# Turning the normalised rows on the DMA queues and VectorE instead of on TensorE

## The reference

```python
h = jnp.maximum(_layernorm(x, axis=-1), 0.0)
x = x + _L0_gnn_ref(h, adj, ...)
h = jnp.maximum(_layernorm(x, axis=-1), 0.0)
x = x + _L1_gnn_ref(h, adj, ...)
# _L0_gnn_ref
Xw = X @ Wv + bv
sj = Xw @ aw[:d, 0]
si = Xw @ aw[d:, 0]
e = jax.nn.leaky_relu(sj[:, None, :] + si[:, :, None] + ab[0], negative_slope=0.2)
alpha_matrix = A * jnp.exp(e)
transition = alpha_matrix / (jnp.sum(alpha_matrix, axis=-1, keepdims=True) + 1e-12)
for k in range(Wk.shape[0]):          # K = 3
    H = H + Xk @ Wk[k] + bk[k]
    Xk = jnp.einsum('bij,bjd->bid', transition, Xk)
return jax.nn.relu(H)
# _L1_gnn_ref: three times  x <- adj @ (x @ W) + b, with relu behind the first two
```

## Time and profile before

| what | value |
|---|---|
| median of 3 runs | 881.63 us (881.37 to 883.54) |
| the profiled execution | 881.72 us, its span 879.9 us |
| PE / PEld busy | 864.7 us (98%) / 817.7 us (93%) |
| DVE busy | 760.2 us (86%) |
| ACT busy | 628.2 us (71%) |
| POOL busy | 435.8 us (50%) |
| DMA queue of SP | 43.81 MB, 20.0% of 16 engines |

### The profile page before, as it was taken

One profiled execution on the slowest core, in us unless ns is written; L12 is line 12 of the kernel. 1 busy time (PEld: TensorE's weight loads), 2 busy tenths in 40 slices (PEclk: granted clock), 3 DMA queues, 4 the chain that ended last, 5 costly groups with the idle time before them and its releaser, 6 DMA issues.

```text
span 879.9 us, 20848 instructions
## 1 busy us (share of the span) xinstructions
PE 864.7 (98%) x6480; PEld 817.7 (93%) x6480; DVE 760.2 (86%) x2001; ACT 628.2 (71%) x1543; POOL 435.8 (50%) x532
## 2 busy tenths in 40 slices
PE   8899999999999999999999999999999999999996
PEld 7799999999999999999999999999999999999996
DVE  5789889889889889889889889899889889889872
ACT  4477777777777777777777777777777777777773
POOL 4454454454454454454454454454454454454452
PEclk9899999999999999999999999999999999999999
DMA  8112122122122122122122122122122122122001
GB/s 202 36 34 57 36 61 56 36 61 56 37 61 57 35 61 56 36 61 57 36 61 58 35 61 57 35 62 56 35 61 57 35 62 57 35 61 58 18 25 37
DMA packets 107869, 46.18 MB, mean 52 GB/s; under 512 B 72560, under 2 KB 107504, under 8 KB 107760
## 3 DMA queue, kind: packets, MB, share of 16 engines
q1 hardware_dynamic: 106672, 43.81, 20.0%
q10 hardware_dynamic: 1088, 1.05, 0.4%
HBM read 28.05 MB, written 16.78 MB: 51 GB/s over the span
## 4 chain that ended last, share of the span: by engine, by line
PE 95%; SPq 1%; POOL 1%; ACT 1%; issue 1%; DMA 1%; DVE 0%; DVEq 0%; ACTq 0%; POOLq 0%
PE bank L856 43%; PE bank_p L856 35%; PE bank_turned L856 7%; PE bank_T L856 5%; PE bank_turned L867 3%; PE bank_T L877 2%; SPq L261 1%; DMA bias_col<-in_L_gnn_b 1%; POOL w_gcn_lo L361 0%; PE bank_p L1012 0%; POOL bias_h L377 0%; ACT h L487 0%; ACT y_full L524 0%; DVE aT_lo L573 0%; SPq L252 0%
## 5 line engine op out<-in xcount | busy, mean ns | idle before, releaser
L334 POOL TENSOR_TENSOR y__lo<-y_full,y__hi 128x256 fp32r<-128x256 f32 x256 | 190.1, 764 | 112.3 <-ACT y_full L524 112.3
L325 POOL TENSOR_TENSOR rstd<-veps,minus_half 128x2 f32<-128x2 f32 x128 | 88.9, 695 | 236.4 <-DVE veps L596 236.4
L856 PE MATMUL bank_p<-w_p_hi,h0T_hi 128*128 128x258 f32 (+1 forms) x512 | 176.3, 360 | 0.1
L856 PE MATMUL bank_p<-w_p_lo,h0T_hi 128*128 128x258 f32 (+1 forms) x512 | 165.3, 339 | 0.0
L856 PE MATMUL bank_p<-w_p_hi,h0T_lo 128*128 128x258 f32 (+1 forms) x512 | 142.1, 339 | 0.7 <-DVE h0T_lo L629 0.7
L856 PE MATMUL bank<-w_gcn_hi,y__hi 128*128 128x256 f32 x512 | 132.8, 292 | 1.5 <-ACT y__hi L524 1.3
L856 PE MATMUL bank<-w_gcn_lo,y__hi 128*128 128x256 f32 x512 | 127.8, 282 | 0.0
L524 ACT ACTIVATE y__hi<-bank,bias_col 128x256 fp32r<-128x256 f32 x256 | 119.7, 467 | 3.0 <-PE bank L856 3.0
L524 ACT ACTIVATE y_full<-bank,bias_col 128x256 f32<-128x256 f32 x256 | 121.6, 475 | 0.0
L350 POOL TENSOR_TENSOR adjT_lo<-adjT_full,adjT_hi 128x256 fp32r<-128x256 f32 x64 | 64.9, 1015 | 82.8 <-ACT adjT_hi L429 82.8
L856 PEld LDWEIGHTS bank_p<-w_p_hi,h0T_hi 128*128 128x128 f32 x512 | 97.3, 190 | 6.2 <-POOL w_p_lo L356 0.3
(11 more groups left out here) (92 smaller groups left out, 2346.2 us busy)
## 6 DMA issues: line engine op xcount, KB each, us to landing
x_in<-in_x SPq DMA_DIRECT2D x64, 256.0 KB, 3.0
x_new<-x_out SPq DMA_DIRECT2D x64, 256.0 KB, 2.2
adj_blocks<-in_adj SPq DMA_DIRECT2D x256, 32.0 KB, 2.3
w_raw<-in_L_gnn_Wk ACTq DMA_DIRECT2D x3, 256.0 KB, 6.9
w_raw<-in_L_gnn_W SPq DMA_DIRECT2D x3, 256.0 KB, 5.5
bk_bc<-in_L_gnn_bk SPq DMA_DIRECT2D x1, 384.0 KB, 6.1
wv_raw<-in_L_gnn_Wv ACTq DMA_DIRECT2D x1, 256.0 KB, 3.8
aw_bc<-in_L_gnn_aw SPq DMA_DIRECT2D x1, 256.0 KB, 5.6
```

The costliest lines, as they stand in the source:

```text
L325: pool.tensor_tensor(rstd[n][k % 2][:], veps[n][k % 2][:], minus_half[:], ALU.pow)\
L334: pool.tensor_tensor(y[n][1][:, c], y_full[n][:, c], plain(y[n][0][:, c]), ALU.subtract)\
L856: return pe.matmul(dst, stationary, moving, start=start, stop=stop, skip_group_check=True)
```

## The change

- `turn_h` and its pair of reads from PSUM stay for the pairs 0 to 2 (`ON_TENSOR = 3`). From pair 3 on, the rows go out to DRAM with one DMA (`write_rows`) and come back in four (`read_rows`) as 32x32 squares in transposed order, pieces of 128 bytes; VectorE turns the insides with one 128x512 transpose (`turn_rows`); ScalarE makes the high part and GpSimd the low part, both in the round before the one that uses them.
- The normalised rows are made by ScalarE (`first_norm`, relu included) two rounds ahead, for which VectorE makes a small `shift(0, ...)`. VectorE's `x_norm` goes. VectorE's 128x512 `hT_low` stays for three pairs only. The moments of x are taken three pairs ahead.
- `attention` moves ahead of `shift(1, b)` on VectorE, `aT_high` ahead of `norm` on ScalarE.
- On TensorE `p2_product` is split: its 8 products with the high part come first in the round, ahead of z3 and ay; the 4 with the low part stay behind ay.
- `x_in` has five slots in place of four, and x is loaded three rounds ahead.

The diff, cut to its core (the waits of unchanged functions and renamed views of PSUM are left out; `low(...)` is a subtraction, dst = src - hi):

```diff
 ROUND = 4
+X_SLOTS = 5
 LAG_B, LAG_C, LAG_D = 1, 2, 3
+ON_TENSOR = 3
...
         rstd = [slots(2, f"rstd{n}_", [P, G]) for n in range(2)]
-        nshift = slots(2, "nshift", [P, G])
-        n0 = slots(2, "n0_", [P, G, D])
+        nshift = [slots(2, f"nshift{n}_", [P, G]) for n in range(2)]
+        h0 = slots(2, "h0_", [P, G, D])
+        h0_rows = [nc.dram_tensor(f"h0_rows{k}", (P, G, D), F32, kind="Internal").ap() for k in range(2)]
+        h0_blocks = slots(2, "h0_blocks", [P, G, C, P])
+        h0T_full = slots(2, "h0T_full", [P, G, C, P])
         h1 = slots(2, "h1_", [P, G, D])
-        h0T = slots_hilo(2, "h0T", [P, C, G, P])
+        h0T = slots_hilo(2, "h0T", [P, G, C, P])
...
+        def early_norm(i):
+            n = i + 1 if i <= 1 else i + 2
+            return n if i >= 1 and n < N_PAIRS else None
+        def late_moments(i):
+            n = 2 if i == 0 else i + 3
+            return n if n < N_PAIRS else None
+        LATE_NORMS = {0: 1, 1: 3}
...
+            def write_rows(i, k):
+                sp.wait_ge(norm_made[0], i + 1)
+                if i >= ON_TENSOR + 2:
+                    sp.wait_ge(rows_landed[k % 2], rows_seen(i - 2))
+                sp.dma_start(h0_rows[k % 2], h0[k % 2][:]).then_inc(rows_out[k % 2], 16)
+            def read_rows(i, k):
+                sp.wait_ge(rows_out[k % 2], 16 * ((i - ON_TENSOR) // 2 + 1))
+                if i >= ON_TENSOR + 2:
+                    sp.wait_ge(rows_turned, i - 2 - ON_TENSOR + 1)
+                pair = h0_rows[k % 2].rearrange("(j r) g (c i s) -> i r (g c) j s", r=SQUARE, c=C, s=SQUARE)
+                for b in range(P // SQUARE):
+                    rows = slice(b * SQUARE, (b + 1) * SQUARE)
+                    sp.dma_start(h0_blocks[k % 2][rows].rearrange("r g c (j s) -> r (g c) j s", s=SQUARE),
+                                 pair[b]).then_inc(rows_landed[k % 2], 16)
...
             def one(i, k):
+                if first(i):
+                    load_x(2)
+                if (n := here(i, -3)) is not None:
+                    load_x(n)
+                turned = here(i, -2) if i >= ON_TENSOR - 2 else None
+                if turned is not None:
+                    write_rows(turned, turned % ROUND)
                 if (n := here(i, -2)) is not None:
-                    load_x(n, (k + 2) % ROUND)
-                    load_adj_blocks(n, (k + 2) % ROUND)
+                    load_adj_blocks(n, n % ROUND)
+                if turned is not None:
+                    read_rows(turned, turned % ROUND)
...
                 pool.tensor_tensor(x1b[k][:], x1[k % 2][:], bias_out[:], ALU.add).then_inc(x1b_made, 1)
+            def hT_low(i, k):
+                pool.wait_ge(hT_hi, i + 1)
+                if after(i, 2):
+                    pool.wait_ge(p01_done, G * (i - 1))
+                hi, lo = h0T[k % 2]
+                pool.tensor_tensor(lo[:], h0T_full[k % 2][:], plain(hi[:]), ALU.subtract).then_inc(hT_lo, 1)
...
                     power(1, b, k - LAG_B)
-                if (n := here(i, -1)) is not None:
-                    power(0, n, k + 1)
+                if (n := LATE_NORMS.get(i)) is not None:
+                    power(0, n, n)
                 if first(i):
                     sum_biases()
                 if c is not None:
                     y_low(1, c, k - LAG_C)
+                if (n := here(i, -1)) is not None and n >= ON_TENSOR:
+                    hT_low(n, n % ROUND)
                 if b is not None:
                     out_bias(b, (k - LAG_B) % ROUND)
+                if (n := late_moments(i)) is not None:
+                    power(0, n, n)
...
+            def first_norm(i, k):
+                act.wait_ge(shift_made[0], i + 1)
+                if i >= ON_TENSOR + 2:
+                    act.wait_ge(rows_out[k % 2], 16 * ((i - 2 - ON_TENSOR) // 2 + 1))
+                elif i >= 2:
+                    act.wait_ge(hT_done, i - 1)
+                for g in range(G):
+                    last = act.activation(h0[k % 2][:, g, :], x_in[i % X_SLOTS][:, g, :], ACT.Relu,
+                                          bias=nshift[0][k % 2][:, g:g + 1], scale=rstd[0][k % 2][:, g:g + 1])
+                last.then_inc(norm_made[0], 1)
+            first_norm(0, 0)
...
-                act.wait_ge(hT_done, i + 1)
+                if i < ON_TENSOR:
+                    act.wait_ge(hT_done, i + 1)
+                else:
+                    act.wait_ge(rows_turned, i - ON_TENSOR + 1)
                 if after(i, 2):
                     act.wait_ge(p01_done, G * (i - 1))
-                act.activation(h0T[k % 2][0][:], turned_ps, ACT.Relu).then_inc(hT_hi, 1)
+                act.activation(h0T[k % 2][0][:], turned_ps if i < ON_TENSOR else h0T_full[k % 2][:], ACT.Copy)\
+                   .then_inc(hT_hi, 1)
...
                     layer_result(0, c)
+                if (n := early_norm(i)) is not None:
+                    first_norm(n, n % ROUND)
...
                     p1_copy(a, k, 0)
+                if a is not None:
+                    aT_high(a, k)
                 if b is not None:
                     norm(b, kb)
-                if a is not None:
-                    aT_high(a, k)
                 if c is not None:
                     layer_result(1, c)
                 if a is not None:
                     p1_copy(a, k, 1)
+                if (n := here(i, -1)) is not None and n >= ON_TENSOR:
+                    hT_high(n, n % ROUND)
...
                     adjT_high(a, k)
+                if (n := LATE_NORMS.get(i)) is not None:
+                    first_norm(n, n % ROUND)
...
                     dve.wait_ge(p01_done, G * (i - 1))
-                dve.scalar_tensor_tensor(lo[:], turned_ps, 0.0, plain(hi[:]), ALU.max, ALU.subtract)\
-                   .then_inc(hT_lo, 1)
+                low(lo[:], turned_ps, hi[:], hT_first_lo)
+            def turn_rows(i, k):
+                dve.wait_ge(rows_landed[k % 2], rows_seen(i))
+                if i >= ON_TENSOR + 2:
+                    dve.wait_ge(hT_hi, i - 1)
+                    dve.wait_ge(hT_lo, i - 1 - ON_TENSOR)
+                dve.transpose(h0T_full[k % 2][:].rearrange("p g c n -> p (g c n)"),
+                              h0_blocks[k % 2][:].rearrange("p g c n -> p (g c n)")).then_inc(rows_turned, 1)
...
                     s3_low(d)
-                if a is not None:
+                if a is not None and a < ON_TENSOR:
                     hT_low(a, k)
+                if (n := early_norm(i)) is not None:
+                    shift(0, n, n % ROUND)
...
                     turn_adj(a, k)
+                if a is not None:
+                    attention(a, k)
                 if b is not None:
-                    shift(b, kb)
-                if nxt is not None:
-                    moments(0, nxt, kn, lambda: attention(a, k))
-                    guard_variance(0, nxt, kn)
-                elif a is not None:
-                    attention(a, k)
+                    shift(1, b, kb)
+                if i == 1:
+                    x_statistics(3, 3)
+                    moments(0, 3, 3, lambda: None)
+                    guard_variance(0, 3, 3)
+                if nxt is not None and nxt >= ON_TENSOR:
+                    turn_rows(nxt, kn)
                 if d is not None:
                     finish(d, kd)
                 if a is not None:
                     aT_low(a, k)
-                if nxt is not None:
-                    x_norm(nxt, kn)
+                if i == 1:
+                    shift(0, 3, 3)
                 if a is not None:
                     guard_sum(a, k)
                     invert_sum(a, k)
-                if (n := here(i, -2)) is not None:
-                    x_statistics(n, (k + 2) % ROUND)
+                if (n := here(i, -3)) is not None:
+                    x_statistics(n, n % ROUND)
                 if a is not None:
                     y1_sum(a, k)
                 if b is not None:
                     m_low(b)
+                if (n := late_moments(i)) is not None:
+                    moments(0, n, n % ROUND, lambda: None)
+                    guard_variance(0, n, n % ROUND)
...
-            def p2_product(i, k):
+            def p2_product(i, k, low):
+                dst = [bank_p2[:, g, 0:D + 2] for g in range(G)]
+                if low:
+                    h_low_ready(i)
+                    times_weights(h0T[k % 2], graph_first, w_p2, dst, range(G), (True,)).then_inc(p2_done, 1)
+                    return
                 pe.wait_ge(hT_hi, i + 1)
                 if first(i):
                     pe.wait_ge(p2_weights_cut, 2)
                 if after(i, 1):
                     pe.wait_ge(y1_made, i)
-                times_weights(h0T[k % 2], w_p2, [bank_p2[:, g, 0:D + 2] for g in range(G)], range(G),
-                              lambda: pe.wait_ge(hT_lo, i + 1)).then_inc(p2_done, 1)
+                times_weights(h0T[k % 2], graph_first, w_p2, dst, range(G), (False,))
...
```

(33 more changed lines are left out.)

96 lines of the change are left out of this document (47 added, 49 removed).

## The result

The changed kernel takes 877.11 us (median of 8 runs, 876.72 to 880.26), the kernel before 882.05 us beside it: ratio 0.995 (95% interval 0.9939 to 0.9961). It is faster by 4.9 us, where 11.4 was forecast. The profiled execution took 879.86 us, a slow one among these 8, against 881.72 before. So the two traces show 1.9 us of the 4.9.

A forecast was written before the change was run, and what follows sets the result against it. Two bounds at once: TensorE's order (13.20 us a round) and a VectorE-TensorE ring (13.11). 881.7 + 3 for the start - 61 x 0.236 (14.4) = 870.3, said as 870.5 us; range 857 to 893 us.

The forecast's parts named there:

- The next pair's `mv` and `veps` leave this stretch: On VectorE, from hb to aT_lo: these two instructions go away from there, in a stretch summed to 6.24 us.
- the ring: Work passing from VectorE (hb to aT_lo) to TensorE (ap to ay) and back each round: 13.11 us before, 12.94 forecast.
- My own walk: GpSimd's instructions timed from hb to see whether x is held: x1b to 10.7 us, fit within 0.1 us.
- the rule on two engines excluding each other: A VectorE instruction with two SBUF inputs and a GpSimd one reading SBUF exclude each other; the second issued is blocked.
- Its VectorE part: VectorE from the start of hb to the end of aT_lo: 6.94 us before, 6.24 forecast.
- The TensorE part: TensorE from the last two ap products to the end of ay: 6.04 - 0.44 + 0.97 = 6.57 us.
- my sign for the whole: TensorE idle about 0.2 us a round before the last ap products; without a wait for aT_lo the prediction fails.
- The forecast round of 12.96: Steady round: the summed 12.94 us, taken as 12.96 for small waits left out, against 13.196 before.
- TensorE's floor: TensorE's own work in a round without the transposes: 13.20 - 0.44 = 12.76 us.
- The rival at 858 us: Chance 0.15: the VectorE-TensorE ring doesn't bind, TensorE's own 12.76 us a round does: 881.7 + 3 - 26.8.
- `x` is not held: VectorE's x free of GpSimd, 0.72 to stats; rival (chance 0.20, including other losses): x stays held, 13.37 a round, 895 us.
- The start: First rounds: GpSimd's late weights 2.0 us, p2's high products waiting for ScalarE's copy 0.9; together 3, between 0 and 6.

The follow-up runs named there:

- Experiment 1: Changed kernel with VectorE's moments of pair i+3 (mv, veps) behind s_lo instead of ahead of it: 868.13 us, ratio 0.9837.
- experiment 4: Changed kernel with VectorE's transpose of the rows behind aT_lo instead of ahead of finish and aT_lo: 876.74 us, ratio 0.9949.
- experiment 9: Changed kernel with ScalarE making pair 1's normalised rows right behind aT_high(0), not at the end of its round 0: 876.88 us, ratio 0.994.
- Experiments 1 and 5: 5, from the changed kernel: moments behind s_lo and rows' transpose behind aT_lo, 867.66 us; moments and p2's high products behind ay, 875.90; all three, 875.34.
- turn twice: Changed kernel with VectorE's 128x512 transpose of the rows done twice, the second into a spare tile: 892.87 us, ratio 1.0114.
- the two kernels with the old order: The kernel before, 882.05 us, and the same with its four transposes left out for pairs 3 to 63, 865.29 us, ratio 0.9809.

## Why the prediction was wrong

The direction and the range were right (chance of faster 0.63), the size was not: 11.4 forecast, 4.9 measured.

**The step that failed** is "The next pair's `mv` and `veps` leave this stretch." I took them off the ring at no cost and did not ask where they went. They went between `m_lo` and `s_lo`, one stretch on, and there GpSimd's `x1b` runs. My own walk had it there, from 9.4 to 10.7 us behind `hb`, where it was measured (9.39 to 10.70). I used the rule on two engines excluding each other for `x`, `y_lo` and `alpha`, and not for an instruction of two elements. It cost 1.1 us a round on VectorE, of which 0.35 reached TensorE. Experiment 1 shows it: 9 us back with that place alone. In the Trainium skill, "SBUF — State Buffer", section "Who interferes with whom", `tensor_scalar` is among the operations that can take the port pair shared with GpSimd, and "issue order, not op shape, decides who blocks". This trace agrees, with 1.26 us for 0.17.

**The ring** was 12.94 in my sum and is 12.77. Its VectorE part is 6.16 (449.94 to 456.10; forecast 6.24). The TensorE part, read off in the same way, is 6.85 with the late `s_lo` in it and 6.53 without (forecast 6.57). Each piece was right to a tenth. The sum was long by 0.02 to 0.04 in five of them (the step from `aT_lo` to `ap`'s products is 0.05, not 0.09). This ring also does not set the round (experiment 4). So my sign for the whole, a wait of TensorE for `aT_lo`, came true and proved nothing: that wait can go and the round stays. The forecast round of 12.96 was near the measured 12.93 of experiment 1, and 870.5 us near its 868.1, for a wrong reason.

**TensorE's floor.** I read 13.20 busy of 13.20 as work. A wait of a tenth doesn't show as idle there, since the modelled ends of the products cover it. By the Trainium skill, "Perfetto Trace Analysis", section "Identifying the Most-Contended Engine", TensorE's matmul occupancy does not measure its headroom; the load of its weights is better. Here the weight loads filled 12.53 of 13.20 before (equal to the floor by chance) and 12.11 of 13.10 after; the trace agrees that TensorE was not full. By the stages, the floor is 12.53, not 12.76. The price of the transposes, 0.44, was right. They take 0.35 from their start to z3's, and z3's first product then costs 0.20 instead of 0.12. That is no wait for `s_lo`, which had ended 0.28 before:

```profile
445.34 0.69 DVE L573 TENSOR_TENSOR s_lo<-bank,s_hi 128x512 fp32r<-128x512 f32 x1 [0.56 <-ACT s_hi L507]
...
456.19 0.36 PE L856 MATMUL bank<-w_gcn_hi,y__hi 128*128 128x256 f32 x1
456.39 0.28 PE L856 MATMUL bank<-w_gcn_lo,y__hi 128*128 128x256 f32 x1
```
The last two lines show the same 0.20 behind m's 128x128 products, and every kernel here has it there (0.20 to 0.22). What I missed is the other 0.23 of 12.76: 0.14 is the pace of s3's and z1's products, which is quicker in the changed kernel, 0.07 a wait for `aT_hi` at the head of `ap`, 0.02 the first `y__lo`. The rival at 858 us thus named the wrong bound: its 12.76 is not TensorE's floor, and that the ring through `aT_lo` is 12.77 is chance. No experiment reached either in its steady rounds.

**What was right.** `x` is not held in the changed kernel (0.69, against 1.12 in the earlier trace rows). `alpha` fits ahead of `nshift` for nothing. The rows' transpose takes 0.70 (forecast 0.71), 0.62 from start to start. TensorE waits 0.23 for `aT_lo` (0.2 forecast). The rows are never late: VectorE waits for none of the 61. `hb` waits 0.34 and not 1, because `veps` filled VectorE's gap (0.91 in the late round, which has no such `veps`). `alpha` was not held by `rstd` (0.43 as ever), so the rule weighed in the prediction does not hold for this pair.

**The start** cost 3.2 us in the two profiled executions (forecast 3), by round 3: s3 and z1 stand at 63.75 for 60.57. That the size fits is luck, since the main reason was another: pair 1's norm stands at the end of ScalarE's first round, so the transposes start at 22.39 (17.49 before), and experiment 9 moves the first `hb` by 2.4 us with that place alone. GpSimd's late weights come on top of this (they end at 28.73, for 25.98) and I did not separate them.

One thing in the start was in no term of mine: TensorE's granted clock. In both profiled executions it is at its lower level, 1.2 GHz, for 6.8 us in the round behind the first `hb` (from 34.28 in the changed kernel, from 31.28 before), so these two can be compared. Experiment 4 is the same program up to its second `hb`, and its trace has the lower clock for 3.41 us at 8.69 and for 3.41 at 22.34. The round behind the first `hb`, and the changed kernel's stretch at the lower clock, then that round in experiment 4:

```profile
26.84:43.08 16.24, 12.24 (x64) 10.30 (x63) 11.76 (x36) 8.89 (x22) 7.62 (x9) 0.79 0.12 28
34.28:41.11 6.83, 5.46 (x26) 4.76 (x24) 4.25 (x15) 3.06 (x7) 3.04 (x4) 0.50 0.18 50
```
```profile
27.37:40.68 13.31, 10.04 (x64) 8.25 (x63) 10.92 (x37) 8.91 (x22) 6.89 (x8) 1.00 0.09 25
```
By the fourth `hb` experiment 4 is 2.4 us ahead (66.78 for 69.22). That is most of the 3 us between the changed kernel's profiled execution and its median. Its other executions left no trace, but six of the eight (876.72 to 877.49) lie near the 876.52 of the profiled execution of experiment 4. So of the 4.9 us between the medians, the traces give some 2 to the new order of instructions; most of the rest goes, as far as these traces show, with where in the start the clock is low, which the prediction knew nothing of. What makes it fall there, no run shows.

**The sum as it was:** from round 3 on, 60 rounds at 13.11 on the average for 13.196 give 5.1 us, less 3.2 at the start: 1.9, as the two profiled executions differ.

What sets 13.11 is a loop through more engines than I followed: from `hb` over ScalarE's norm and y, GpSimd's `y__lo`, `h0T_lo`, `x1b`, then `veps`, `s_lo`, z3 and `ay`. `x1b` starts 9.39 us after `hb` in the changed kernel and in experiment 4 alike. With the hold gone, a second loop of 12.93 decides, 0.16 above the one through `aT_lo`. Experiments 1 and 5 show that it reaches TensorE at `y__lo`. The links of both loops other than `veps` and `s_lo` are read from the traces and not tested singly.

## What to carry to other kernels

When an instruction leaves a critical stretch, follow it to its new place and ask there the same questions, whom it is queued ahead of and which engine runs beside it; its size is no excuse. A tuned pipeline can have several loops of nearly one length, as here 13.11, 12.93 and 12.77 us. So price a change by the second and third loop, and add no losses of different ones. Take an engine's own work from the least distance between starts of each stage, over several rounds or kernels, and not from its busy time. Compare kernels round for round, and look at the granted clock of the start before a difference of 3 us between medians is put down to an edit. The best complete version is the changed kernel with the moments behind `s_lo` and the rows' transpose behind `aT_lo` or not (867.7 and 868.1 us, the same within their measurement).

## What the runs showed of the hardware

- A VectorE addition on 128x2 elements took 0.17 us alone and 1.23 to 1.28 us when it was issued just behind the start of GpSimd's 128x512 addition, to that one's end (0.80 in "turn twice", where it was issued later).
- GpSimd waits too: its 128x2 power took 0.70 alone and 1.07 issued behind VectorE's `y_lo`, a 128x256 subtraction 0.70 to 0.74 alone and 1.05 or 1.26, `x1b` 1.31 and 1.74. Yet `alpha` (0.43), issued 0.4 us into GpSimd's power of 0.69, took no longer.
- Behind 128x128 products TensorE's first 128x256 product cost 0.20 us to the next one, where 0.12 is usual, in every kernel. z1's products stood 0.120 apart in the two kernels with the old order and 0.114 to 0.118 in the others.
- A stretch of 6.83 us at a granted clock of 0.50 stood in a round of 16.24 us that took 13.31 without it.
- Two rounds of the changed kernel took 13.45 us. The kernel without the DRAM trip has the same two, so they aren't its doing; I have no cause.
